# Second attention's weighted values with the tokens on partitions

## The chip, the cores and the metric

The kernel runs on one core of one Trainium2 chip. The metric is the device time of the whole program, in microseconds, the median of several runs. The same program was also run once under the profiler; all rows below are of that one execution.

## The reference

The program takes x (64 sequences of 64 tokens with 128 features, so 4096 tokens) and a context of the same length with 96 features. It adds four layers to x, each on a normalised x: a first attention with a long convolution, a first set of eight experts with two chosen per token, a second attention, and a second set of experts. The change lies in the second attention:

```
qh = (q @ Wq + bq)  -> 16 heads of 8 features
kh = (kv @ Wk + bk) -> 16 heads of 8
vh = (kv @ Wv + bv) -> 16 heads of 8
scores = einsum('bhqd,bhkd->bhqk', qh, kh) * scale
attn = softmax(scores, axis=-1)
out = einsum('bhqk,bhkd->bhqd', attn, vh)   # b, 64 tokens, 16 heads, 8
return out.reshape(b, 64, 128) @ Wo + bo
```

Each of the 64 sequences attends to its own 64 context rows. The layer that follows chooses two of eight experts for each token from logits that the attention's result goes into, so the kernel computes these choices in the same loop, block by block of four tiles.

## The kernel before

The function `combination_and_second_attention` works on 32 tiles of 128 tokens (two sequences each, called b). The engines have their own instruction streams, written out by hand, and meet by semaphores only. Each stream runs a function `slot_of(x)` once for each tile number t (`march`), and inside a slot it works on different tiles, so that the stages of the attention overlap: `a` is tile t+3 (its queries and keys), `g` is tile t+1 (scores, softmax, values), `x` is tile t (its softmax rows are turned), `c` is tile t-1 (weighted values), `d` is tile t-2 (projection and sum).

In one slot, in order:

- TensorE: the scores of g in two halves (L1864; the second half waits for the ScalarE exponentials of the slot before, L2017, as they read the same PSUM tile); the projections of queries and keys of a (L1874, L1875) and of the values of g (L1880), all into the PSUM tile `psx`; in slots 0 to 3 also four small matmuls of logits (L1842); `attend(c)`; once in four slots `ranks` (L1924); `project(d)` (L1931); `turn(x)`, eight transposes of the softmax numerators (L1939).
- ScalarE: the exponentials of g's first half (L2012), the copies of a's keys and queries from `psx` (L2032, L2033), the two copies of g's values into `vb` (L2038), which wait for `attend(c)` because c and g share a `vb` buffer, the exponentials of the second half (L2015, L2017), in some slots the rows for the experts (L2021), and the copies of the turned numerators into `pt` (L2065).
- VectorE: maximum and difference of both halves of g's scores (L2221, L2230), statistics (L2266), `normalise(c)`, which is a reciprocal (L2272) and a product (L2274), `add_result(d)` (L2292), and then, by the slot's number, work on the choice of experts: I call the slots by it. C (t = 3 modulo 4) makes the first choice, D (t = 0) the second, A (t = 1) places the tokens, B (t = 2) has little.
- GpSimd: masked keys for a (L1791), constants, roots, and the indirect DMAs of the expert rows (L1809).

`attend(c)` has the values as the stationary operand: for each of the two sequences and eight pairs of heads a matmul with 32 columns of `vb` (two heads' values in a block of zeros) and 64 columns of `pt` moving, which gives features on partitions. Eight more matmuls with blocks of ones make the sums of the softmax, repeated over the features, in a further 128 columns of the PSUM tile `pso`. `normalise` inverts all 128 x 128 sums and multiplies. Since the result has features on partitions it is at once the stationary operand of the projection.

`normalise(c)` waits not only for `attend(c)` but also for the projection of d in the same slot (`after(dve, s["y"], min(c.t, NT - 2))`), since both use the PSUM tile `pso`. `fill(pe, G, out, n)` elsewhere in the kernel runs n matmuls of a zero tile (128 x 128 with 256 columns moving, L192) whose result nobody reads.

## Time and profile before

| | us |
|---|---|
| median of 3 runs | 920.45 |
| the three runs | 912.15, 920.45, 920.72 |
| the profiled execution | 909.81 |
| its span | 908.6 |
| part of the span with the loop's projections (start of the first in the loop to start of the last) | 572.97 to 735.50 |

The span is the time from the first to the last instruction of the profiled execution; the device time holds 1.2 us more. TensorE is busy in 78% of the span, VectorE in 75%, GpSimd in 62% and ScalarE in 52%, but these are averages over stages with different limits, so the loop is read by itself below. The profiled execution is 1.2% shorter than the median of the three runs, which themselves differ by 0.9%.

### The profile page before, as it was taken

Reading aid. Unit: us, or ns where it says so; the run is one execution under the profiler, and the core shown is the slowest. Engines: PE = TensorE matmul, PEld = TensorE weight load, DVE = VectorE, ACT = ScalarE, POOL = GpSimd, SP = SyncE. Lnnn points to the kernel's source line nnn. Section 1 sums busy time; section 2 is a strip of 40 time slices with the busy share of each in tenths; the row PEclk is TensorE's granted clock in tenths of the full one; section 3 lists DMA queues with packets and bytes.
Section 4 is the critical chain, followed back from the end, with each engine's and each line's share of the span. In section 5 each row is a group of like instructions: output and inputs, shape, how many; then the busy total and the mean of one; then the engine's idle time right before and its main releaser. Section 6 shows DMA issues by size and latency. Waiting matters only on the chain. (4 is left out here: it accounts for less than half of the span.)

```text
span 908.6 us, 21071 instructions
## 1 busy us (share of the span) xinstructions
PE 707.4 (78%) x6384; PEld 522.0 (57%) x6384; DVE 677.9 (75%) x3212; ACT 472.4 (52%) x1318; POOL 565.0 (62%) x932
## 2 busy tenths in 40 slices
PE   0697898899888899943798269988888865899960
PEld 0364565566686566422575256666666642799960
DVE  6798999999447887686111294798998886699964
ACT  3466666765303554520233464777777741677740
POOL 7688977786647443201777684347777767377770
PEclk9879999998999999976899655998988876899985
DMA  6300123777227877500564500000000013799918
GB/s 147 59 25 9 41 49 63 90 93 100 41 47 282 268 253 253 180 1 7 76 122 114 181 28 1 3 2 23 23 26 25 23 34 118 212 274 266 266 53 277
DMA packets 98830, 94.43 MB, mean 104 GB/s; under 512 B 37511, under 2 KB 82302, under 8 KB 98142
## 3 DMA queue, kind: packets, MB, share of 16 engines
q1 hardware_dynamic: 91268, 79.34, 33.1%
q0 software_dynamic: 6592, 13.58, 6.0%
q8 instruction: 52, 0.85, 0.4%
q14 instruction: 60, 0.49, 0.3%
q10 hardware_dynamic: 858, 0.17, 0.1%
HBM read 47.76 MB, written 43.19 MB: 100 GB/s over the span
## 5 line engine op out<-in xcount | busy, mean ns | idle before, releaser
L2455 POOL DMA_INDIRECT expert_pairs<-e_ys,e_home x78 | 75.4, 967 | 38.4 <-issue 23.5
L1791 POOL TENSOR_SCALAR a_kb<-a_kr,a_m,a_bk 128x128 f32<-128x128 f32 x128 | 57.8, 452 | 44.4 <-ACT a_kr L2032 32.3
L1809 POOL DMA_INDIRECT expert_slots<-r_rows,r_slotu x64 | 63.3, 990 | 30.2 <-DVE r_rows L2189 15.1
L961 DVE MATCH_REPLACE8 work<-m,work 128x64 f32<-128x64 f32 x384 | 75.6, 206 | 0.0
L1533 POOL DMA_INDIRECT ex_rows<-rows,slot_source x32 | 30.7, 961 | 53.3 <-POOLq L1176 43.9
L948 DVE MAX8 m<-work 128x8 f32<-128x64 f32 x384 | 57.0, 208 | 0.0
L1864 PE MATMUL a_pss<-a_kb,a_qt 32*64 32x256 f32 x512 | 41.5, 463 | 13.8 <-ACT a_pp L2017 11.7
L2221 DVE TENSOR_REDUCE a_mx<-a_pss 128x8 f32<-128x512 f32 x64 | 43.8, 685 | 8.1 <-PE a_pss L1864 7.8
L2422 PE MATMUL e_ps<-e_XH,e_wh 128*128 128x256 f32 x156 | 48.1, 308 | 1.5 <-DVE e_XL L2467 1.5
L1585 ACT ACTIVATE ex_hs<-ex_psh,vec 128x512 f32<-128x512 f32 x32 | 22.0, 687 | 49.8 <-PE ex_psh L1566 49.1
L2424 PE MATMUL e_ps<-e_XH,e_wl 128*128 128x256 f32 x156 | 44.6, 286 | 0.0
L2423 PE MATMUL e_ps<-e_XL,e_wh 128*128 128x256 f32 x156 | 44.6, 286 | 0.0
L2012 ACT ACTIVATE a_pp<-a_dd 128x512 f32<-128x512 f32 x32 | 20.2, 630 | 45.3 <-DVE a_dd L2230 45.3
L1939 PE MATMUL a_psp<-ident,a_pp 128*128 128x128 f32 x256 | 39.5, 306 | 1.9 <-ACT a_pt L2065 1.9
L2272 DVE RECIPROCAL a_rt<-a_pso 128x128 f32<-128x128 f32 x31 | 29.5, 950 | 14.8 <-PE a_pso L1931 11.9
L209 POOL TENSOR_SCALAR mlp_ln_v<-mlp_ln_mv 128x4 f32<-128x4 f32 x24 | 5.5, 228 | 55.7 <-DVE mlp_ln_mv L201 55.7
L1358 ACT ACTIVATE rt_rs<-mlp_psh,vec 128x512 f32<-128x512 f32 x32 | 22.0, 687 | 34.7 <-PE mlp_psh L1307 34.7
L1543 POOL DMA_INDIRECT planes<-ex_ys,slot_home x32 | 31.2, 975 | 9.9 <-issue 9.4
L834 PE MATMUL psf<-filmw,us 97*128 97x512 f32 x64 | 37.2, 666 | 0.0
L2230 DVE TENSOR_TENSOR a_dd<-a_mx,a_pss 128x512 f32<-128x512 f32 x64 | 35.5, 554 | 2.2
L2065 ACT ACTIVATE a_pt<-a_psp 128x512 f32<-128x512 f32 x64 | 35.4, 610 | 2.2 <-PE a_psp L1939 2.1
L1939 PEld LDWEIGHTS a_psp<-ident,a_pp 128*128 128x128 f32 x256 | 34.8, 161 | 2.5 <-ACT a_pp L2017 2.1
(477 smaller groups left out, 2469.5 us busy)
## 6 DMA issues: line engine op xcount, KB each, us to landing
expert_slots<-rt_unfilled SPq DMA_DIRECT2D x151, 130.0 KB, 2.6
ahead<-folded_weights SPq DMA_DIRECT2D x20, 386.0 KB
e_wf<-folded_weights SPq DMA_DIRECT2D x19, 386.0 KB, 4.1
planes<-rt_zeros SPq DMA_DIRECT2D x4, 1024.0 KB
ew<-in_L_ffn_ew SPq DMA_DIRECT2D x16, 256.0 KB, 3.8
pair_y<-expert_pairs SPq DMA_DIRECT2D x16, 256.0 KB, 5.2
e_xr<-expert_slots SPq DMA_DIRECT2D x27, 130.0 KB, 3.2
folded_weights<-fold_done SPq DMA_DIRECT2D x8, 384.0 KB, 4.3
```

Source lines behind the costliest of these rows:

```text
L834: pe.matmul(psf[:], us[j][:], G.filmw[:], start=True, stop=True).then_inc(s["film"], 1)
L948: mx = dve.max(m8[x.j][:, h, r, :], src[:, h, :])
L961: return own.did(dve.match_replace(wk_[x.j][:, h, :], m8[x.j][:, h, r, :], src[:, h, :], TAKEN))
L1791: m = pool.tensor_scalar(kb[a.j][:, :, h, :], k, m4[:, h:h + 1], bk4[:, h:h + 1], ALU.mult, ALU.add)
L1809: pool.indirect_dma_start(G.slots, bass.IndirectOffsetOnAxis(ap=slot[:, b, k, t:t + 1], axis=0), rb[b % NB][:, k, t, :], None).then_inc(se ...
L1864: mm = pe.matmul(pss[half][T * b:T * b + T, h, 0:HG * T], qt[g.j][rows, T * b:T * b + T], kb[g.j][rows, b, :, :], start=True, stop=True)
L1939: mm = pe.transpose(psp[half][:, k, :], pp[x.j][:, h:h + 2, :].rearrange("p h k -> p (h k)"), G.ident[:])
L2221: dve.tensor_reduce(m, scores(half), AX.X, ALU.min).then_inc(s["lowest"], 1)
L2422: pe.matmul(psh[m][c][:], wh[j][:, m, c, :], XH[j][:], start=True, stop=False)
L2423: pe.matmul(psh[m][c][:], wh[j][:, m, c, :], XL[j][:], start=False, stop=False)
L2424: pe.matmul(psh[m][c][:], wl[j][:, m, c, :], XH[j][:], start=False, stop=True).then_inc(h_ps[m][c], 1)
L2455: pool.indirect_dma_start(G.pair, bass.IndirectOffsetOnAxis(ap=home[i % NY][:, k:k + 1], axis=0), ys[i % NY][:, k, :], None).then_inc(kept ...
```

## The change

The weighted values are made with the softmax numerators as the stationary operand (64 columns, the tokens of one sequence) and 18 columns moving: eight values for each of two heads, and two columns of ones, each over the 64 context rows of one of the heads. 16 matmuls give tokens on partitions, and the two sums of each pair of heads stand beside the values. The eight matmuls of ones are gone. The reciprocal is of 128 x 16 numbers and the product spreads each over eight features. For the projection the result must be turned back: TensorE transposes it in the next slot (`turn_out(d)`, into columns 384 to 511 of `psx`) and ScalarE copies it to a new buffer (`keep_out(d)`), behind its copies of the values of g. `project(d)` waits for that copy. Ahead of `attend(c)` two `fill` matmuls are added. ScalarE's first copies from `psx` also wait for `turn_out(d)`. At the loop's end the order on VectorE changes a little: the last `normalise` stands ahead of `place(LAST - 1)`.

```diff
--- before.py
+++ after.py
@@ -1624,13 +1624,13 @@
         bqs, neg = (C.sb("a1_" + n, [P, 1], ctx=ctx) for n in ("bqs", "neg"))
         m4 = C.sb("a1_m4", [P, HG], ctx=ctx)
         bk4 = C.sb("a1_bk4", [P, HG], ctx=ctx)
-        ones = C.sb("a1_ones", [P, 2, 2, 2, DH1], ctx=ctx)
-
-        vb = two("vb", [P, 2 * NP * 32])
+        VW = 2 * DH1 + 2
+
+        vb = two("vb", [P, 2 * NP, VW])
         qt, kr, kb = two("qt", [P, P]), two("kr", [P, P]), two("kb", [P, 2, HG, T])
         mx, dd, pp = two("mx", [P, H1]), two("dd", [P, H1, T]), two("pp", [P, H1, T])
         pt = two("pt", [P, NP, P])
-        rt, of = two("rt", [P, P]), two("of", [P, P])
+        rt, of, turned_of = two("rt", [P, NP, 2]), two("of", [P, P]), two("ofT", [P, P])
         rb = [C.sb(f"r2_rows{j}", [P, 2, TB, ROW], ctx=ctx) for j in range(NB)]
         full = {n: C.sb("r2_" + n, [P, NT] + k, ctx=ctx) for n, k in (
             ("st", [6]), ("mv", [2]), ("v", []), ("nm", []), ("rstd", []), ("shift", []), ("mc", [NE]), ("lg", [NE]), ("e", [NE]), ("idx", []),
@@ -1669,7 +1669,7 @@
         psl = pso[:, 480:480 + TB * NE]
         s = {n: C.sem("a1_" + n) for n in (
             "ready", "zero", "qkv", "based", "v_sb", "q_sb", "k_sb", "kb",
-            "scores", "lowest", "centred", "exp", "turned", "turned_sb", "inverse", "o", "of", "y", "x", "pool")}
+            "scores", "lowest", "centred", "exp", "turned", "turned_sb", "inverse", "o", "of", "of_turned", "of_sb", "y", "x", "pool")}
         r = {n: C.sem("r2_" + n) for n in (
             "iota", "lg", "var", "root", "rows", "d", "exp", "sel", "ranks", "pos", "counted",
             "slot", "gs", "gturned", "gt", "bias", "bias_sum", "dve", "table")}
@@ -1680,11 +1680,9 @@
         first_weights = [C.later_sem(f"e1_first_weights{i}") for i in range(WEIGHTS_AHEAD)]
         sent = [C.queue_sem(f"r2_sent{j}") for j in range(NB)]
 
-        def vb_rows(j, odd):
-
-            whole = vb[j][:]
-            return bass.AP(whole.tensor, whole.offset + T * odd * whole.ap[0][0] + DH1 * odd,
-                           [[whole.ap[0][0], T], [64, NP], [48, 2], [1, DH1]])
+        def summed(c):
+
+            return outcome(c.t)[:, 0:NP * VW].rearrange("p (k w) -> p k w", w=VW)
 
         def tiles(b):
             return slice(b * TB, (b + 1) * TB)
@@ -1748,10 +1746,9 @@
                 pool.sem_inc(s["zero"], 1)
                 for j in range(2):
                     step.then(pool.memset(vb[j][:], 0.0))
-                step.then(pool.memset(ones[:], 0.0))
-                for pair in range(2):
+                for j in range(2):
                     for odd in range(2):
-                        step.then(pool.memset(ones[T * odd:T * odd + T, pair, pair, odd, :], 1.0))
+                        step.then(pool.memset(vb[j][T * odd:T * odd + T, :, 2 * DH1 + odd:2 * DH1 + odd + 1], 1.0))
                 pool.sem_inc(s["zero"], 1)
                 pool.iota(home_i[:], pattern=[[B * T, 2], [1, NT]], base=0, channel_multiplier=NT).then_inc(r["iota"], 1)
                 pool.iota(tile_i[:], pattern=[[1, NTILE]], base=0, channel_multiplier=0).then_inc(r["iota"], 1)
@@ -1865,6 +1862,7 @@
                                                    kb[g.j][rows, b, :, :], start=True, stop=True)
                             mm.then_inc(s["scores"], 1)
                     if a.real() or g.real():
+                        after(pe, s["of_sb"], d.t)
                         after(pe, s["q_sb"], min(a.t, NT))
                         after(pe, s["v_sb"], min(g.t, NT))
                         if a.real():
@@ -1881,6 +1879,8 @@
                                                    G.ctxT[:, g.t * P + T * b:g.t * P + T * b + T], heads[:, odd],
                                                    start=True, stop=True)
                         mm.then_inc(s["qkv"], 1)
+                    if d.real():
+                        turn_out(d)
                     ranked = due(x, PLACE)
                     if c.real() or ranked is not None:
                         after(pe, cm["base"], min(FIRST + x.t, NBLK))
@@ -1890,6 +1890,7 @@
                     if 0 <= x.t < NBLK - FIRST:
                         base_logits(FIRST + x.t)
                     if c.real():
+                        fill(pe, G, pso[:, 0:2 * P], 2)
                         attend(c)
                     if ranked is not None:
                         ranks(ranked)
@@ -1904,19 +1905,16 @@
                 def attend(c):
                     pe.wait_ge(s["turned_sb"], 2 * c.t + 2)
                     pe.wait_ge(s["v_sb"], c.t + 1)
-                    out = outcome(c.t)
-                    for b in range(2):
-                        for odd in range(2):
-                            for i in range(4):
-                                k = 2 * i + odd
-                                mm = pe.matmul(out[32 * i:32 * i + 32, T * b:T * b + T],
-                                               vb[c.j][:, 32 * (NP * b + k):32 * (NP * b + k) + 32],
-                                               pt[c.j][:, k, T * b:T * b + T], start=odd == 0, stop=odd == 1)
-                    for odd in range(2):
-                        for i in range(4):
-                            mm = pe.matmul(out[32 * i:32 * i + 32, P:2 * P], ones[:, odd].rearrange("p s o d -> p (s o d)"),
-                                           pt[c.j][:, 2 * i + odd, :], start=odd == 0, stop=odd == 1)
+                    out = summed(c)
+                    for k in range(NP):
+                        for b in range(2):
+                            mm = pe.matmul(out[T * b:T * b + T, k, :], pt[c.j][:, k, T * b:T * b + T], vb[c.j][:, NP * b + k, :],
+                                           start=True, stop=True)
                     mm.then_inc(s["o"], 1)
+
+                def turn_out(d):
+                    pe.wait_ge(s["of"], d.t + 1)
+                    pe.transpose(psx[:, 384:512], of[d.j][:], G.ident[:]).then_inc(s["of_turned"], 1)
 
                 def ranks(b):
                     pe.wait_ge(r["sel"], b + 1)
@@ -1926,9 +1924,9 @@
                               start=False, stop=True).then_inc(r["ranks"], 1)
 
                 def project(d):
-                    pe.wait_ge(s["of"], d.t + 1)
+                    pe.wait_ge(s["of_sb"], d.t + 1)
                     out = result(d.t)
-                    pe.matmul(out, of[d.j][:], wo[:], start=True, stop=True).then_inc(s["y"], 1)
+                    pe.matmul(out, turned_of[d.j][:], wo[:], start=True, stop=True).then_inc(s["y"], 1)
 
                 def turn(x):
                     for half in range(2):
@@ -1948,13 +1946,18 @@
                 march(slot_of, -1, NT - 1)
                 t0, t1, t2, t3 = (Tile(t, t // 2, t % 2, True) for t in range(NT - 4, NT))
                 turn(t3)
+                pe.wait_ge(s["v_sb"], NT)
+                pe.wait_ge(s["of_sb"], t1.t)
+                turn_out(t1)
                 pe.wait_ge(s["centred"], 2 * NT)
                 project(t1)
                 pe.wait_ge(s["x"], t0.t + 1)
                 attend(t2)
                 attend(t3)
                 ranks(LAST - 1)
+                turn_out(t2)
                 project(t2)
+                turn_out(t3)
                 pe.wait_ge(s["x"], t1.t + 1)
                 project(t3)
                 pe.wait_ge(s["turned_sb"], 2 * NT)
@@ -2024,8 +2027,11 @@
                 def slot_of(x):
                     a, g = x.by(3), x.by(1)
                     exp(g, 0)
+                    d = x.by(-2)
                     if a.real() or g.real():
                         act.wait_ge(s["qkv"], x.t + 4)
+                        if d.real():
+                            act.wait_ge(s["of_turned"], d.t + 1)
                     if a.real():
                         after(act, s["scores"], 2 * (a.t - 1))
                         after(act, s["kb"], a.t - 1)
@@ -2034,9 +2040,11 @@
                     if g.real():
                         after(act, s["o"], g.t - 1)
                         for odd in range(2):
-                            v = psx[T * odd:T * odd + T, 256:384].rearrange("p (k c d) -> p k c d", c=2, d=DH1)
-                            m = act.activation(vb_rows(g.j, odd), v, ACT.Copy)
+                            v = psx[T * odd:T * odd + T, 256:384].rearrange("p (k d) -> p k d", d=DH1)
+                            m = act.activation(vb[g.j][T * odd:T * odd + T, :, DH1 * odd:DH1 * odd + DH1], v, ACT.Copy)
                         m.then_inc(s["v_sb"], 1)
+                    if d.real():
+                        keep_out(d)
                     if due(x, PLACE) is not None:
                         second_gate(due(x, PLACE))
                     exp(g, 1)
@@ -2064,6 +2072,11 @@
                         act.wait_ge(s["turned"], 2 * x.t + half + 1)
                         act.activation(pt[x.j][:, 4 * half:4 * half + 4, :], psp[half][:], ACT.Copy).then_inc(s["turned_sb"], 1)
 
+                def keep_out(d):
+                    act.wait_ge(s["of_turned"], d.t + 1)
+                    after(act, s["y"], d.t - 1)
+                    act.activation(turned_of[d.j][:], psx[:, 384:512], ACT.Copy).then_inc(s["of_sb"], 1)
+
                 def second_gate(b):
                     act.wait_ge(r["d"], b + 1)
                     act.activation(part(b)["d"], part(b)["d"], ACT.Exp).then_inc(r["exp"], 1)
@@ -2084,15 +2097,20 @@
                 march(slot_of, -1, NT - 1)
                 t0, t1, t2, t3 = (Tile(t, t // 2, t % 2, True) for t in range(NT - 4, NT))
                 keep_turned(t3)
+                keep_out(t1)
                 for b in (LAST - 1, LAST):
                     act.wait_ge(r["root"], b + 1)
                     after(act, sent[b % NB], 2 * TB * 16 * (b // NB))
                     keep_rows(b, 0)
                     keep_rows(b, 1)
                     second_gate(b)
+                    if b < LAST:
+                        keep_out(t2)
                     keep_rows(b, 2)
                     keep_rows(b, 3)
                     keep_places(b)
+                    if b < LAST:
+                        keep_out(t3)
                 for half in range(2):
                     act.wait_ge(r["gturned"], half + 1)
                     act.activation(gt[:, 4 * half:4 * half + 4, :], psp[1][:], ACT.Copy).then_inc(r["gt"], 1)
@@ -2266,12 +2284,15 @@
                     step.did(dve.bn_stats(full["st"][:, n.t, :], G.X[:, n.t, :]))
 
                 def normalise(c):
-                    out = outcome(c.t)
+                    out = summed(c)
                     dve.wait_ge(s["o"], c.t + 1)
                     after(dve, s["y"], min(c.t, NT - 2))
-                    dve.reciprocal(rt[c.j][:], out[:, P:2 * P]).then_inc(s["inverse"], 1)
+                    after(dve, s["of_turned"], c.t - 1)
+                    dve.reciprocal(rt[c.j][:], out[:, :, 2 * DH1:VW]).then_inc(s["inverse"], 1)
                     dve.wait_ge(s["inverse"], c.t + 1)
-                    TT(of[c.j][:], out[:, 0:P], rt[c.j][:], ALU.mult).then_inc(s["of"], 1)
+                    each = [P, NP, 2, DH1]
+                    TT(of[c.j][:].rearrange("p (k o d) -> p k o d", o=2, d=DH1), out[:, :, 0:2 * DH1].rearrange("p k (o d) -> p k o d", o=2),
+                       wide(rt[c.j][:].unsqueeze(3), each), ALU.mult).then_inc(s["of"], 1)
 
                 def means(b):
 
@@ -2307,8 +2328,8 @@
                 add_result(t1)
                 normalise(t2)
                 place_ranks(LAST - 1)
+                normalise(t3)
                 place(LAST - 1)
-                normalise(t3)
                 add_result(t2)
                 for n in (t0, t1, t2):
                     statistics(n)
```

## Rows read from the trace of the kernel before

**Rows 1.** The page, part 2: granted TensorE clock in 40 slices, in tenths.

```profile
PEclk9879999998999999976899655998988876899985
```

**Rows 2.** A round of four slots: us, busy us (instructions) per engine, clock, DMA, GB/s.

```profile
683.44:707.34 23.90, 21.22 (x350) 15.30 (x349) 21.13 (x64) 17.68 (x56) 18.26 (x29) 0.86 0.08 25
```

**Rows 3.** Waits in the loop (566 to 745 us): total us, times, longest.

```profile
DVE a_rt L2272 <- PE a_pso L1931: 11.9, 16, 1.4
```

**Rows 4.** Timeline, slots B and C: start us, us, engine, line, operation [idle before].

```profile
688.10 0.63 ACT L2012 ACTIVATE a_pp<-a_dd 128x512 f32<-128x512 f32 x1 [2.17 <-DVE a_dd L2230]
689.13 0.55 ACT L2038 ACTIVATE a_vb<-a_psx 64x128 f32<-64x128 f32 x2
690.99 0.66 PE L1864 MATMUL a_pss<-a_kb,a_qt 32*64 32x256 f32 x8 [0.67 <-ACT a_pp L2017]
691.58 0.49 PE L1874 MATMUL a_psx<-XF,a_wq 128*128 128x128 f32 x2
692.22 0.45 PE L1880 MATMUL a_psx<-a_wv,ctxT 96*64 96x64 f32 x8
692.60 0.65 PE L1912 MATMUL a_pso<-a_pt,a_vb 128*32 128x64 f32 x32
693.01 0.26 ACT L2032 ACTIVATE a_kr<-a_psx 128x128 f32<-128x128 f32 x1
693.62 0.50 PE L1931 MATMUL a_pso<-a_wo,a_of 128*128 128x136 f32 x2
693.76 0.55 ACT L2038 ACTIVATE a_vb<-a_psx 64x128 f32<-64x128 f32 x2
693.85 0.92 PEld L1939 LDWEIGHTS a_psp<-ident,a_pp 128*128 128x128 f32 x8
694.23 0.96 DVE L2272 RECIPROCAL a_rt<-a_pso 128x128 f32<-128x128 f32 x1 [0.53 <-PE a_pso L1931]
694.93 0.21 PEld L1864 LDWEIGHTS a_pss<-a_kb,a_qt 32*64 32x64 f32 x8 [0.16 <-issue]
695.22 0.29 DVE L2274 TENSOR_TENSOR a_of<-a_pso,a_rt 128x128 f32<-128x128 f32 x1
697.37 0.69 DVE L2221 TENSOR_REDUCE a_mx<-a_pss 128x8 f32<-128x512 f32 x1
```

**Rows 5.** Timeline, slots A and D: VectorE's product and its next maximum.

```profile
684.68 0.29 DVE L2274 TENSOR_TENSOR a_of<-a_pso,a_rt 128x128 f32<-128x128 f32 x1
686.65 0.69 DVE L2221 TENSOR_REDUCE a_mx<-a_pss 128x8 f32<-128x512 f32 x1
700.93 0.29 DVE L2274 TENSOR_TENSOR a_of<-a_pso,a_rt 128x128 f32<-128x128 f32 x1
703.85 0.68 DVE L2221 TENSOR_REDUCE a_mx<-a_pss 128x8 f32<-128x512 f32 x1
```

**Rows 6.** Timeline, TensorE: 64 matmuls with 64 columns stationary between fills (first layer's convolution).

```profile
262.37 0.51 PE L192 MATMUL conv_unread<-still 128*128 128x256 f32 x2
262.81 2.06 PE L1047 MATMUL psy<-XM,toe 64*64 64x32 f32 x64
```

**Rows 7.** Timeline, slot t = 2: logits and values on TensorE, full clock.

```profile
570.96 1.06 PE L1842 MATMUL a_pso<-e_wgt,XF 128*128 128x8 f32 x8
571.95 0.65 PE L1912 MATMUL a_pso<-a_pt,a_vb 128*32 128x64 f32 x32
```

**Rows 8.** The projection's line by itself: ns shortest/median/longest, first and last start in us.

```profile
L1931 PE MATMUL a_pso<-a_wo,a_of x58: 279/383/596, 573.0 to 735.7; 128*128 128x136 f32 x58
```

**Rows 9.** Windows of 1 us around a fall and the next rise of TensorE's clock.

```profile
701.00:702.00 1.00, 0.29 (x8) 0.21 (x8) 0.93 (x6) 1.00 (x4) 0.69 (x2) 1.00 0.18 62
703.00:704.00 1.00, 0.44 (x13) 0.34 (x16) 0.90 (x6) 0.69 (x2) 0.80 (x3) 0.68 0.21 67
710.00:711.00 1.00, 1.00 (x16) 0.67 (x10) 0.90 (x5) 0.00 (x0) 0.00 (x0) 0.91 0.00 0
```

**Rows 10.** Timeline, a small reciprocal in slot A.

```profile
686.16 0.18 DVE L2186 RECIPROCAL r_gate<-r_q 128x4 f32<-128x4 f32 x1
```

**Rows 11.** Timeline, behind the loop: the last reciprocal.

```profile
745.39 0.96 DVE L2272 RECIPROCAL a_rt<-a_pss 128x128 f32<-128x128 f32 x1
```

## The prediction

> **What bounds the kernel now.** I read the page's clock line first, then windows over the loop of the second attention, then its waits, then the timeline of four slots. The clock line [rows 1] shows that the loop (slices 24 to 32) runs at nearly full clock, so the change can't gain by waking TensorE. A round of four slots takes 23.90 us [rows 2], 5.98 a slot, and VectorE is busy for 21.13 of it, TensorE for 21.22: two engines close to their limit. What VectorE lacks is mostly one wait: its 128 x 128 reciprocal stands behind the projection of the same slot, 11.9 us in 16 slots [rows 3]. In slot C one sees it: the projection starts at 693.62 and lasts 0.50, the reciprocal starts at 694.23, 0.11 after its end [rows 4]. Otherwise VectorE runs through: in slot D from its product (700.93) straight to the next maximum (703.85) [rows 5]. So today the loop is VectorE's, with TensorE's projection as the second hand in A and C. The 29 projections of the loop start between 573.0 and 735.5 [rows 8]: 28 intervals, 162.5 us, 5.80 each.
>
> **What the change takes from VectorE.** The reciprocal shrinks from 128 to 16 elements per partition. It takes 0.96 for 128 [rows 4] and 0.18 for 4 [rows 10]; linear between them, 16 take 0.25. With the 0.03 to the product's start that is 0.28 in place of 0.99, 0.7 less per slot. The product keeps its 128 elements and its 0.29. The engine with the most work is relieved by 21 us over 30 slots. What matters is whether it is still the one waited for.
>
> **What it puts on TensorE's path.** The projection used to follow `attend` at once. Now it waits for `keep_out`, which on ScalarE stands behind the two value copies, and these wait for `attend(c)` of the same slot. TensorE works in order, so it stands still through both copies, and the next slot's transposes, scores and projections queue behind it. I add up one round of TensorE, from projection start to projection start, at full clock:
> - projection to the transposes 0.23 (693.62 to 693.85); transposes to the next scores 1.08 (to 694.93); two halves of scores at 0.59 (690.99 to 691.58), 1.18; queries and keys 0.64 (to 692.22); values 0.38 (to 692.60) [rows 4];
> - `turn_out`: two records; the transposes' eight take 0.92 [rows 4], so a quarter, 0.23;
> - the two fills: 0.44 from their start to the next narrow matmul (262.37 to 262.81), in which both changes between full and 64-column matmuls lie [rows 6];
> - the new `attend`: 16 matmuls are 32 records, as the old values' were. The nearest row is the convolution's: 64 records with 64 stationary columns, 2.06 [rows 6]; half is 1.03, and the hop to ScalarE is 0.06, so 1.1;
> - value copies and `keep_out`: the copies take 0.55 [rows 4]; `keep_out` has the shape and source of the key copy, 0.26 [rows 4]; together 0.80, and 0.06 to TensorE, 0.86.
>
> The sum is 0.23 + 1.08 + 1.18 + 0.64 + 0.38 + 0.23 + 0.44 + 1.1 + 0.86 = 6.14. The same sum today is 4.5: no stall, no turn, no fills, and 1.02 for `attend` (692.60 to 693.62 [rows 4]).
>
> Bounds of `attend`, the one large unknown: below, the old values' 32 records, which four column groups share, are all done in 0.65 [rows 7], giving 0.7 and a round of 5.75. Above, if loads of 64 columns don't overlap, half of what full-width loads with 8 columns moving take: 8 records in 0.99 (570.96 to 571.95 [rows 7]), 0.124 each, so 32 x 0.062 = 2.0, with the hop 2.1 and a round of 7.14. I stay with 1.1, since the convolution's form is nearest (same columns, few moving, f32).
>
> The values' records of today come at 0.65 / 32 = 20 ns [rows 7]. The Trainium skill ("TensorE: Matmul & The Clock Gate", section "Wait — 56ns, not 53.3ns?") says that matmuls never start closer than about 25 ns, however few columns move; by that figure `attend` would be 32 x 25 = 0.80, an estimate from that page, and the total 2.4 us less. This trace does not show that floor.
>
> Against the change speaks another rule. What a row shows is 0.65 for values in groups of 32 columns [rows 7]. The Trainium skill ("TensorEngine Tiling (Array Packing)", section "Theoretical Speedup") gives operands of up to 32 columns a factor of four and those of up to 64 only two; twice 0.65 is 1.3, an estimate by that rule, and the total would be 3.7 us more. No run here shows it yet.
>
> **VectorE's path in the new order.** It too passes through the projection, now with ScalarE in it. From a projection's start: its end 0.50, reciprocal 0.11, to the product 0.28, then the stretch X from the product to the next slot's maximum; from there 1.45 to the first exponential (686.65 [rows 5] to 688.10), 1.03 to the value copies (689.13), 0.86 to the next projection [rows 4]: 4.23 + X. X is 1.97 in A (684.68 to 686.65), 2.92 in D [rows 5], 2.15 in C (695.22 to 697.37) [rows 4]. That gives A 6.20, C 6.38, D 7.15; B has no such work and stays below TensorE's round. Both paths run from projection to projection, so each interval is the larger: A 6.20, B 6.14, C 6.38, D 7.15, a round of 25.87 against 23.90. The gain in the reciprocal is spent: VectorE waits longer for the projection than it saves.
>
> **The sum.** Interval 2 to 3 carries the four logit matmuls, 6.14 + 0.99 = 7.13; then four plain ones 24.56; one C 6.38; five rounds 129.35; a D and an A 13.35. Together 180.8 against 162.5: +18.3 (low end +14.4, high end +38.5, by the same sum with 5.75 and 7.14).
> - Slot 1 has no projection yet: its fills, 0.4, ends 0 and 0.5.
> - Behind the loop VectorE is alone for long: two reciprocals, the last at 745.39 with 0.96 [rows 11], save 0.7 each: -1.4. There the added turns and copies fall beside the placing work on VectorE, which now follows the last product; if that cover is gone they cost 1.
> - Clock. It falls once a round, in the slot where TensorE was idle most (busy 0.29 and 0.44 of two of the microseconds before, clock then 0.5) and is back at 710.1, 6.4 us later [rows 9]. Today VectorE hides most of that; with TensorE on the path a fall at the same place would double A's `attend`, turn and fills (1.03 + 0.67, of which D's slack of 7.15 - 6.14 takes 1.0) and its projection and transposes (0.2 + 0.92): about 1.8. Six falls: 10.5; none: 0. The stall now leaves TensorE idle 0.9 of 6.1 in every slot and 1.9 of 7.2 in D, and the fills add work, so the pause is rarer than the one that now precedes a fall; I take 3, nearer to none.
> - Memsets at the start (no 512-wide ones, four thin ones): nothing, as GpSimd is then in the block of sums long before. The waits of ScalarE's key copy for `turn_out(d)`: nothing, the turn is issued right behind the values' matmuls; in B it may be late by 0.2, inside TensorE's round. No DMA is added or moved; GpSimd (18.26 of 23.90 busy [rows 2]) only gets longer slots.
>
> 18.3 + 0.4 - 1.4 + 3 = +20.3. On the profiled execution's 909.8 this is 930.1. That execution lies 10.6 below the median of the runs, 920.45, so on the median it is 941.
>
> **The rivals.**
> - **VectorE stays the bound** (faster). If TensorE's round were under 5.3 (5.98 less 0.7), each slot would shed the reciprocal's 0.7: -21, with the tail -22, 898. For it: 21.13 of 23.90 busy. Against it: five terms of the round without `attend` already give 5.0, and VectorE's own wait is on that projection. 0.07.
> - **No change that can be told.** `attend` at its low end and each hop 0.1 shorter than the rows, 56 hops: 14.4 - 1.0 - 5.6 = +8, 928. 0.13.
> - **Narrow loads don't overlap.** Round 7.14: 38.5 - 1.0 = +37.5, 958. For it: full-width loads are what sets 0.124 today. Against it: the convolution's 0.032. 0.12.
> - **The clock sinks.** The stall in every slot keeps TensorE at half clock in half of the slots. TensorE's own terms, 6.14 - 0.86 = 5.3, would at most double; halfway, +2.5, in 14 slots is 35 more, 976. For it: the stall is new in all slots, and the fall in [rows 9] needed only a few idle stretches. 0.10.
> - That the change doesn't do what it says, say a reciprocal that stays at 0.96, would leave the same stall and add 0.7 to VectorE's path in A, C and D, +12 on the forecast; the row of 0.18 speaks against it. It is within the range and in the forecast's chance.
>
> **How the numbers follow.** Forecast 0.58. A measurement of this kernel can tell about 1% (9.2 us) from no change. Slower by more takes in the forecast, narrow loads and the clock: 0.79. Within 1%: 0.14. Faster: 0.07. The range goes from 922 (low end on a run near the fastest, 912 + 13 = 925, and a part of the second rival) to 963 (past the narrow loads' 958); outside are the faster case and most of the clock's.
>
> **What would show it.** Right: ScalarE's `keep_out` starts right behind the value copies, the projection starts 0.8 to 0.9 after the values' copies began, TensorE's largest wait is that copy; the reciprocal takes about 0.25 and VectorE waits over 1 us ahead of it in nearly every slot; `attend` takes 1.0 to 1.1; a round is 25.9. Wrong: a round at or below 23.9, VectorE without waits, or a projection that starts before the value copies end. A granted clock under 0.8 in the loop would show the fourth rival.

## The result and the profile after

The changed kernel takes 976.3 us (median of four runs, 960.4 to 985.0), the kernel before 917.1 (four runs, 912.2 to 920.7): the ratio is 1.053, with a 95% interval of 1.039 to 1.066. A second set of runs on another occasion gave 975.8 against 921.2, ratio 1.063 (1.054 to 1.071). The ratios leave out runs in a slower state (beside h1 to h4 that is 17 of the 29 runs of the kernel before, whose other 12 have a median of 918.5), so they are not the quotients of the medians. The forecast was 941, which is 2.2% above the kernel before, with a range to 963: the direction was right, the size too small, as 5.3% and 6.3% were measured.

The page of the changed kernel, its clock line and three lines of its part 5 (operation, count | busy us, mean ns | idle before, releaser):

```profile
PEclk9797898979859999965998556787776776799995
L2291 DVE RECIPROCAL a_rt<-a_pso 128x16 f32<-128x16 f32 x31 | 8.0, 258 | 60.8 <-issue 53.7
L1929 PE MATMUL a_pso<-a_wo,a_ofT 128*128 128x136 f32 x58 | 19.5, 432 | 34.8 <-ACT a_ofT L2078 34.5
L1911 PE MATMUL a_pso<-a_vb,a_pt 128*64 128x18 f32 x992 | 40.0, 226 | 0.0
```

The reciprocal has shrunk to 258 ns as forecast. The clock line answers [rows 1]: the loop, slices 24 to 32 before, now shows 6 to 8 where it showed 7 to 9, and the projection L1929 has 34.8 us of idle time ahead of it, ended by the copy of the turned rows.

A round of four slots in the changed kernel, from projection to projection of slot D, by windows (columns as in [rows 2]):

```profile
702.04:732.66 30.62, 25.91 (x296) 20.28 (x297) 19.05 (x64) 18.72 (x60) 18.18 (x30) 0.72 0.06 19
```

30.62 us against 23.90 in [rows 2], with the clock at 0.72. VectorE has 19.05 us of work where it had 21.13, so it sheds 2.1 us and idles 11.6.

The waits of the changed kernel from 566 to 800 us, against [rows 3]:

```profile
DVE a_rt L2291 <- issue: 50.1, 26, 3.6
PE a_pso L1929 <- ACT a_ofT L2078: 33.3, 24, 2.8
DVE a_mx L2239 <- PE a_pss L1861: 25.1, 20, 2.5
```

VectorE's wait ahead of the reciprocal has gone from 11.9 us to 50.1 (put down to "issue", but it ends right behind the projection, 0.09 us in the timeline below). Its wait for scores is 25.1 us; in the kernel before it was at most the 7.8 us of the page's line:

```profile
L2221 DVE TENSOR_REDUCE a_mx<-a_pss 128x8 f32<-128x512 f32 x64 | 43.8, 685 | 8.1 <-PE a_pss L1864 7.8
```

The timeline of slot C at full clock and of the next one, D, which runs at half clock, in the changed kernel:

```profile
692.26 0.14 PEld L1917 LDWEIGHTS a_psx<-ident,a_of 128*128 128x128 f32 x1
692.27 0.36 PEld L192 LDWEIGHTS a_pso<-still 128*128 128x128 f32 x2
692.76 1.11 PE L1911 MATMUL a_pso<-a_vb,a_pt 128*64 128x18 f32 x32
692.89 0.63 ACT L2015 ACTIVATE a_pp<-a_dd 128x512 f32<-128x512 f32 x1 [1.91 <-DVE a_dd L2248]
693.93 0.56 ACT L2044 ACTIVATE a_vb<-a_psx 64x128 f32<-64x128 f32 x2
694.51 0.28 ACT L2078 ACTIVATE a_ofT<-a_psx 128x128 f32<-128x128 f32 x1
694.93 0.47 PE L1929 MATMUL a_pso<-a_wo,a_ofT 128*128 128x136 f32 x2 [1.05 <-ACT a_ofT L2078]
695.49 0.26 DVE L2291 RECIPROCAL a_rt<-a_pso 128x16 f32<-128x16 f32 x1 [1.37 <-issue]
696.20 0.69 PE L1861 MATMUL a_pss<-a_kb,a_qt 32*64 32x256 f32 x16
696.82 0.49 PE L1872 MATMUL a_psx<-XF,a_wq 128*128 128x128 f32 x2
698.34 1.11 PE L1911 MATMUL a_pso<-a_vb,a_pt 128*64 128x18 f32 x32
700.01 0.63 ACT L2015 ACTIVATE a_pp<-a_dd 128x512 f32<-128x512 f32 x1 [2.16 <-DVE a_dd L2248]
701.62 0.28 ACT L2078 ACTIVATE a_ofT<-a_psx 128x128 f32<-128x128 f32 x1
702.04 0.79 PE L1929 MATMUL a_pso<-a_wo,a_ofT 128*128 128x136 f32 x2 [2.58 <-ACT a_ofT L2078]
704.47 1.16 PE L1861 MATMUL a_pss<-a_kb,a_qt 32*64 32x256 f32 x16
706.18 0.69 DVE L2239 TENSOR_REDUCE a_mx<-a_pss 128x8 f32<-128x512 f32 x1
708.17 1.90 PE L1911 MATMUL a_pso<-a_vb,a_pt 128*64 128x18 f32 x32
710.12 0.56 ACT L2044 ACTIVATE a_vb<-a_psx 64x128 f32<-64x128 f32 x2 [1.34 <-PE a_pso L1911]
710.70 0.28 ACT L2078 ACTIVATE a_ofT<-a_psx 128x128 f32<-128x128 f32 x1
711.12 0.79 PE L1929 MATMUL a_pso<-a_wo,a_ofT 128*128 128x136 f32 x2
```

Up to 695 it is what [rows 4] would give with the edit: `attend` 1.11, value copies from 693.93, `keep_out` from 694.51, projection at 694.93. But the projection at 702.04 starts 2.6 us after `attend` is done (698.34 and 1.11): it waits for the copy (701.62), which stands behind an exponential (700.01) that waited for VectorE. From there on everything on TensorE takes almost twice as long, and the next projection comes 9.08 us later.

The distance between projections, split over the run, and where it lies: windows from the first of the loop's 28 intervals to the end of the last, in the kernel before (its second profile) and the changed kernel.

```profile
581.02:744.22 163.20, 143.91 (x2436) 103.96 (x2432) 143.85 (x423) 119.47 (x367) 107.98 (x178) 0.90 0.06 19
```

```profile
601.87:809.48 207.61, 173.79 (x2069) 135.93 (x2069) 128.23 (x425) 127.78 (x398) 108.11 (x177) 0.74 0.05 15
```

So 163.2 us (162.5 in the first profile) became 207.6: +45 between the first profiles, and +46 between the second profiles of both (209.6). Between the second profiles 13.2 us more lie ahead of the loop (581.0 and 594.2 to its first projection), in code that is the same (below). The part behind the 28 intervals is 1 us shorter (173.1 to 172.1), which answers the -1.4 of the forecast.

### The profile page after: what moved, and what is told of

The parts are those of the page before. It is cut to its first block and busy times, and to the rows that moved or that the text cites. A ratio compares the mean times of both kernels' runs of the same rounds, so it can differ in the third digit from the quotient of the medians.

```text
span 981.6 us, 20322 instructions
## 1 busy us (share of the span) xinstructions
PE 760.5 (77%) x5964; PEld 573.8 (58%) x5964; DVE 660.2 (67%) x3212; ACT 481.1 (49%) x1350; POOL 563.9 (57%) x931
## 5 line engine op out<-in xcount | busy, mean ns | idle before, releaser
L1937 PE MATMUL a_psp<-ident,a_pp 128*128 128x128 f32 x256 | 51.4, 368 | 0.4 <-ACT a_pt L2073 0.4
L2291 DVE RECIPROCAL a_rt<-a_pso 128x16 f32<-128x16 f32 x31 | 8.0, 258 | 60.8 <-issue 53.7
L1929 PE MATMUL a_pso<-a_wo,a_ofT 128*128 128x136 f32 x58 | 19.5, 432 | 34.8 <-ACT a_ofT L2078 34.5
L1937 PEld LDWEIGHTS a_psp<-ident,a_pp 128*128 128x128 f32 x256 | 45.8, 198 | 0.7 <-issue 0.6
L1911 PE MATMUL a_pso<-a_vb,a_pt 128*64 128x18 f32 x992 | 40.0, 226 | 0.0
L1911 PEld LDWEIGHTS a_pso<-a_vb,a_pt 128*64 128x64 f32 x992 | 36.9, 157 | 4.9 <-issue 1.8
```

The costliest lines, as they stand in the source:

```text
L1911: mm = pe.matmul(out[T * b:T * b + T, k, :], pt[c.j][:, k, T * b:T * b + T], vb[c.j][:, NP * b + k, :], start=True, stop=True)
L1937: mm = pe.transpose(psp[half][:, k, :], pp[x.j][:, h:h + 2, :].rearrange("p h k -> p (h k)"), G.ident[:])
```

## The experiments

In the table, "intervals" are the 28 distances between projections in the profile, "clock" is the granted clock over them, and the times are medians beside the kernel before on the same chip. The ratio is of the changed version to the kernel before.

| version | us | before | ratio (95%) | intervals | clock |
|---|---|---|---|---|---|
| kernel before, second profile | 918.5 | 918.3 | | 163.2 | 0.90 |
| changed kernel again | 975.8 | 921.2 | 1.063 (1.054 to 1.071) | 209.6 | 0.73 |
| e1: copy at the head of ScalarE's slot | 920.5 | 921.2 | 1.003 (0.996 to 1.011) | 161.1 | 0.92 |
| e2: changed, no fills | 982.5 | 921.2 | none | 211.5 | 0.68 |
| e3: before, with the wait alone | 959.3 | 921.2 | none | 188.5 | 0.84 |
| f1: changed, three value buffers | 963.4 | 918.7 | 1.042 (1.035 to 1.049) | 200.4 | 0.77 |
| f2: f1 without fills | 957.9 | 918.7 | 1.041 (1.034 to 1.049) | 195.8 | 0.70 |
| f3: changed, eight fills in the stall | 965.9 | 918.7 | 1.053 (1.043 to 1.063) | 193.5 | 0.85 |
| f4: before, three value buffers | 917.0 | 918.7 | 0.998 (0.996 to 1.001) | 163.3 | 0.87 |
| g4: changed, transposes ahead of the projection | 963.5 | 918.3 | 1.040 (1.032 to 1.047) | 196.5 | 0.74 |
| g2: e1 with three value buffers | 926.8 | 918.3 | 1.009 (1.005 to 1.012) | 160.4 | 0.91 |
| g3: e1 without fills | 924.3 | 918.3 | 1.006 (1.003 to 1.010) | 159.1 | 0.91 |
| h1: changed, more fills ahead of the convolution | 967.0 | 926.8 | 1.047 (1.040 to 1.053) | 209.6 | 0.73 |
| h3: before, the same | 921.1 | 926.8 | 1.007 (1.002 to 1.011) | 162.7 | 0.88 |
| h2: g2, the same | 916.7 | 926.8 | 0.992 (0.987 to 0.997) | 162.2 | 0.90 |
| h4: h2 without the fills of the loop | 921.1 | 926.8 | 0.998 (0.993 to 1.002) | 162.8 | 0.89 |

**Is it the change, and which part?** The theory: the projection now hangs on ScalarE's copies, TensorE stands still for them, and its clock falls. The rival: the added work on TensorE (turn, fills, matmuls with 64 columns).

The changed kernel again:

> The changed kernel once more, beside runs of the kernel before on the same chip. In its first profile 28.9 us of the 73 us by which the spans differ lie ahead of the loop's first projection, where nothing that costs time was changed, and the loop's projections are 42 us further apart. If the change alone were the cause, the part ahead of the loop would again be 25 to 29 us longer. If that part is a matter of the single run (a clock that falls at other places), it is within 10 us of 573 here, and the total is 30 to 50 us above the kernel before. The intervals between projections should again be some 7.1 in most slots and 5.6 only where the clock is full.

The loop repeats (209.6), and so does the part ahead: the first projection is at 594.2. Neither case written down fits it: it is 21 us later than 573, and 13 later than in the second profile of the kernel before.

The copy moved to the head of ScalarE's slot (e1):

```diff
+                    d = x.by(-2)
+                    if d.real():
+                        keep_out(d)
                     exp(g, 0)
-                    d = x.by(-2)
...
                         m.then_inc(s["v_sb"], 1)
-                    if d.real():
-                        keep_out(d)
```

> The copy of the turned rows moved to the head of ScalarE's slot, ahead of the first exponential and of the copies of the values, so that the projection no longer waits for copies that wait for the weighted values of the same slot. Theory of the stall: TensorE's round loses 0.9 us and its clock holds; VectorE keeps the gain of its small reciprocal; the loop's round of four slots comes to 21 to 24 us and the total within -20 to +5 us of the kernel before, 40 us or more below the changed kernel. Rival, the added work on TensorE (turn, fills, matmuls of 64 columns): the stall was only slack, and the time stays within 10 us of the changed kernel.

920.5 against 921.2: the whole loss of 55 us is gone with all of the added work still in place. In the loop the intervals fall from 209.6 to 161.1; about 10 of the 55 us are a clock ahead of the loop (below). The rival falls: the place of the copy makes the loop's loss, not the added work. The forecast here was the kernel before -20 to +5, and it came out at its upper part. A round of the loop at full clock, and its timeline in slot C:

```profile
671.22:693.44 22.22, 20.92 (x298) 15.47 (x298) 18.60 (x65) 18.74 (x59) 18.35 (x30) 1.00 0.09 27
```

```profile
681.43 0.28 ACT L2078 ACTIVATE a_ofT<-a_psx 128x128 f32<-128x128 f32 x1 [1.06 <-PE a_psx L1917]
681.56 1.11 PE L1911 MATMUL a_pso<-a_vb,a_pt 128*64 128x18 f32 x32
681.60 0.62 ACT L2015 ACTIVATE a_pp<-a_dd 128x512 f32<-128x512 f32 x1
682.61 0.50 PE L1929 MATMUL a_pso<-a_wo,a_ofT 128*128 128x136 f32 x2
682.72 0.56 ACT L2046 ACTIVATE a_vb<-a_psx 64x128 f32<-64x128 f32 x2
```

22.2 us in place of 23.9, with the clock at 1.00 throughout. The copy (681.43 and 0.28) is done 0.15 us after `attend` has begun, the projection (682.61) follows `attend` at once, and the value copies come after it.

The changed kernel without the two fills (e2, the line is left out):

> The changed kernel without the two fill matmuls. Theory of the stall: with the stall in place the fills cost 0.25 to 0.44 us a slot at full clock but keep TensorE a little busier; without them the clock falls as often or more often, the total within 15 us of the changed kernel, either way. Theory of the added work: 0.25 to 0.44 us less at full clock and twice that at half, 30 slots: 10 to 20 us faster.

Within 7 us (982.5, but single runs lie from 964 to 991), the clock of the loop at 0.68 in place of 0.73 and its intervals 2 us longer: less work on TensorE brought nothing that can be told.

The wait alone, in the kernel before (e3):

```diff
                         after(pe, s["x"], d.t)
+                        after(pe, s["v_sb"], min(g.t + 1, NT))
                         project(d)
```

> The kernel before with one part of the change alone: TensorE's projection waits for the copies of the values in the same slot, as it does in the changed kernel by way of the copy behind them. No turn, no fills, no narrow matmuls; the big reciprocal and the ones stay. Theory of the stall: TensorE stands still for 0.65 us in each slot and VectorE's path from projection to projection grows by it: A 6.6, B 5.2, C 6.8, D 7.6 at full clock, a round of 26.3 in place of 23.9, 17 us, and with the clock falling more often 25 to 45 us. Rival, the added work: no more than 5 us above the kernel before.

+38 on the median, +25 in the intervals, with the clock down from 0.90 to 0.84. The profiled run is the shortest of the four (942.6; the others take 958 to 963), so what the others add is not seen. At full clock its slots take 6.54 (A), 5.48 (B), 6.69 (C) and 7.61 (D), within 0.3 of the numbers written down beforehand (C takes 7.39 and 7.71 in two rounds). One wait, without any new work, makes more than half of the loop's loss.

**Which wait inside the chain?** Three buffers for the values take away ScalarE's wait for `attend` of the same slot (f1):

```diff
-        vb = two("vb", [P, 2 * NP, VW])
+        vb = [C.sb(f"a1_vb{j}", [P, 2 * NP, VW], ctx=ctx) for j in range(3)]
...
-                        after(act, s["o"], g.t - 1)
+                        after(act, s["o"], g.t - 2)
...
-                            m = act.activation(vb[g.j][...
+                            m = act.activation(vb[g.t % 3][...
```

> The changed kernel with three buffers for the values in place of two, so that ScalarE's copies of the values, and the copy of the turned rows behind them, no longer wait for the weighted values of the same slot; the order of all instructions stays. Theory of the stall: the wait for attend goes, TensorE stands still at most where VectorE's centred scores are late, the round of four slots falls from about 30 to 22 to 24 us and the 28 intervals from 208 to 150 to 165; the total is 40 to 60 us below the changed kernel and within 10 us of the kernel before. Rival, the added work on TensorE: nothing changes by more than 10 us.

This was wrong: 963.4, intervals 200.4. The timeline of f1 shows why:

```profile
692.49 1.11 PE L1911 MATMUL a_pso<-a_vb,a_pt 128*64 128x18 f32 x32
693.38 0.69 DVE L2248 TENSOR_TENSOR a_dd<-a_mx,a_pss 128x512 f32<-128x512 f32 x1
694.10 0.63 ACT L2015 ACTIVATE a_pp<-a_dd 128x512 f32<-128x512 f32 x1 [2.09 <-DVE a_dd L2248]
695.14 0.55 ACT L2044 ACTIVATE a_vb<-a_psx 64x128 f32<-64x128 f32 x2
695.72 0.28 ACT L2078 ACTIVATE a_ofT<-a_psx 128x128 f32<-128x128 f32 x1
696.14 0.53 PE L1929 MATMUL a_pso<-a_wo,a_ofT 128*128 128x136 f32 x2 [2.53 <-ACT a_ofT L2078]
```

`attend` is done at 693.60, yet the projection waits until 696.14: the copy stands behind the first exponential (694.10), which is released by VectorE's difference (693.38), which VectorE reaches only after the last projection. That is the path I had summed as 4.23 + X. The wait for `attend` was not what bound it.

The same without fills (f2):

> As the one before and without the two fills. If the clock holds by itself once TensorE no longer stands still, the slots that TensorE bounds lose the 0.3 us of the fills: 5 to 9 us below the version with fills. If the fills are what holds the clock, it falls more often and the total is 5 to 30 us above that version.

957.9, 5.5 less at the edge of telling, and a clock of 0.70: neither side is clear.

TensorE's transposes ahead of the projection (g4), so that it has work in the stall:

```diff
-                    if d.real():
-                        after(pe, s["x"], d.t)
-                        project(d)
                     if x.real():
                         ...
                         turn(x)
+                    if d.real():
+                        after(pe, s["x"], d.t)
+                        project(d)
```

> The changed kernel with the eight transposes of the softmax numerators issued ahead of the projection in each slot, so that TensorE has 1.1 us of its own work in the stall. If TensorE's standing still is what costs (through its round, 5.57 us at full clock, and through the clock), the intervals fall from 208 to 165 to 185 and the total by 25 to 45 us. If the path through VectorE and ScalarE is the bound (normalise, maximum, exponential, copies, projection: 6.15, 6.35 and 7.36 in slots A, C and D at full clock), these intervals stay, only B and the early slots gain 0.6 each, 6 us, and what else is gained is clock: 185 to 205.

The second case: intervals 196.5, slots A and C no shorter than in the changed kernel (6.36 at a clock of 0.87, and 6.25 to 7.30 at full clock), the early ones 5.31 in place of 5.57. So it is the ring projection, VectorE, ScalarE, projection that binds in A, C and D, and TensorE's own round only in B and the early slots. But the clock did not come back with the work in the stall. The loops of g4 and of e3, which has the wait and no new work (busy us: TensorE, its loads, VectorE, ScalarE, GpSimd; then the clock):

```profile
599.89:796.39 196.50, 183.05 (x2069) 139.90 (x2069) 126.28 (x425) 124.52 (x397) 108.20 (x177) 0.74 0.05 16
578.49:766.99 188.50, 142.17 (x2432) 106.78 (x2433) 145.66 (x425) 120.20 (x369) 108.86 (x177) 0.84 0.05 17
```

TensorE is busy in 93% of g4's loop at 0.74, and in 75% of e3's at 0.84. So the clock does not follow TensorE's busy share alone, and what in the new order holds it down stays open.

**How much is clock?** Eight more fills in the stall (f3):

```diff
                         after(pe, s["x"], d.t)
+                        for _ in range(8):
+                            pe.matmul(pso[:, NP * VW:2 * P], G.still[:, 0:P],
+                                      G.still[:, 0:2 * P - NP * VW], start=True, stop=True)
                         project(d)
```

> The changed kernel with its stall, and eight more fill matmuls (112 columns moving, into columns of the PSUM tile that nobody reads) in the stall, ahead of the projection. They take about 0.9 us at full clock, as long as the stall. If the clock is the larger part of the loss, the granted clock of the loop rises from 0.74 to over 0.9, the 28 intervals fall from 208 to 175 to 185 (my blind sum without falls gave 181) and the total by 20 to 35 us. If the waiting alone is the loss, whatever the clock, the intervals stay over 200. Where the clock does fall, the fills take 1.8 us and cost up to 0.9 a slot, so 208 to 225.

The clock rose to 0.85 and the intervals fell to 193.5, 14 to 16 less: about half of what was expected, as the clock still fell in D and A (intervals of 10.60, 9.45 and 9.75 at half clock, where the fills cost double). It shows the slots at full clock, though. Intervals with a granted clock of 0.95 or more, in the changed kernel's two profiles and in f3, beside the forecast's:

| slot | forecast | at full clock | at half or mixed, changed kernel |
|---|---|---|---|
| A | 6.20 | 6.07 to 6.18 | 7.13 to 9.09 |
| B | 6.14 | 5.51 to 5.58 | 7.01 to 7.96 |
| C | 6.38 | 6.26 to 7.46 | 7.11 to 7.56 |
| D | 7.15 | 7.36 (one, in f3) | 7.10 to 9.09 |

C has two values. In 15 of the 18 C slots of these three profiles one short VectorE operation takes 0.5 to 1.2 us more than it takes elsewhere, beside GpSimd's addition of the constant, and these slots take 7.06 to 7.56; the three without it take 6.26, 6.30 and 6.35. Two of them in f3, and one in the changed kernel:

```profile
643.91 1.34 POOL L1779 TENSOR_TENSOR X<-X,e_cst 128x544 f32<-128x544 f32 x1
643.93 1.37 DVE L2171 TENSOR_TENSOR r_e<-r_e,iota 128x32 f32<-128x32 f32 x1
700.93 1.34 POOL L1779 TENSOR_TENSOR X<-X,e_cst 128x544 f32<-128x544 f32 x1
700.99 1.32 DVE L2178 SCALAR_TENSOR_TENSOR r_lg<-r_oh,r_lg 128x32 f32<-128x32 f32 x1
```

```profile
696.25 1.33 POOL L1779 TENSOR_TENSOR X<-X,e_cst 128x544 f32<-128x544 f32 x1
696.58 1.06 DVE L2168 TENSOR_TENSOR r_e<-r_lg,r_m 128x32 f32<-128x32 f32 x1
```

With these the 28 intervals at full clock come to 175 to 182 (five early ones at 5.6 with 1 for the logits, six A, five B, six C at 6.3 to 7.3, six D at 7.36), against 163 before. So by this estimate +12 to +19 is the path, and the other 26 to 33 of the 45 are the clock. As nearly every C slot of the changed kernel is a long one, 19 and 26 are the nearer ends. The 163 of the kernel before holds falls of its own (its clock is 0.90), so this compares the changed kernel at full clock with the kernel before as it ran.

Three value buffers in the kernel before (f4):

> The kernel before with three buffers for the values and nothing else of the change. VectorE, with 21.1 of 23.9 us busy in a round, is the bound there, so the theory expects no gain beyond the waits of VectorE for the projection, 0 to 8 us below the kernel before. If the order of the copies was a hidden cost of the kernel before as well, it gains 10 us or more.

917.0 against 918.7: nothing that can be told, which agrees with VectorE as the bound of that loop.

**What lies ahead of the loop?**

> The kernel before, profiled a second time. Its first profile is the only one of ten that reaches the loop's first projection by 573 us; the other kernels' lie at 578 to 602, although their code ahead of the loop is the same. If that part is a matter of the run, this profile lies at 578 to 590 (and some 5 to 15 us of the difference between the first two profiles are no effect of the change); if the changed layout costs there, it lies at 573 again. The 28 intervals of the loop are 162 to 164 either way.

581.0: the first profile of the kernel before was 8 us early at this point by its run. But the changed kernel's 594 and 602 are later still, and one line accounts for it. The convolution of the first layer, L1047, same code in all: durations ns, first to last start, in the second profile of the kernel before, the changed kernel, and h1.

```profile
L1047 PE MATMUL psy<-XM,toe x512: 218/227/248, 258.3 to 277.1; 64*64 64x32 f32 x171
```

```profile
L1047 PE MATMUL psy<-XM,toe x512: 218/291/313, 259.1 to 290.9; 64*64 64x32 f32 x171
```

```profile
L1047 PE MATMUL psy<-XM,toe x512: 218/227/248, 259.9 to 278.8; 64*64 64x32 f32 x171
```

In the changed kernel it takes 31.8 us at a granted clock of 0.53, before 18.8 at 1.00. It does so in both profiles of the changed kernel and in e2, f1, f2, g2 and g4; in both of the kernel before, e1, e3, f3, f4 and g3 it does not. In all seven of the first kind the clock falls 1.9 to 2.8 us after the convolution's start and stays at half for 34 us. More fills ahead of it (h1, and h3 in the kernel before):

```diff
-                fill(pe, G, psa[0][:, 0:256], 12)
+                fill(pe, G, psa[0][:, 0:256], 30)
```

> The changed kernel with 30 in place of 12 fill matmuls between the first layer's attention and its convolution. In both profiles of the changed kernel the clock falls 3 us into the convolution, which then takes 31 us in place of 19. If that fall is a part of the measured difference, the convolution is back at 19 us, the total 10 to 13 us below the changed kernel's 976, at 960 to 966, less up to 2 us for the added fills. If the convolution's clock in a profile says nothing on the timed runs, the total stays at 970 to 978.

967.0, 9 below the changed kernel, a little above the range written down, and the convolution is back at 18.9 us, with the loop's intervals unchanged at 209.6: this clock is a part of the measured difference.

> The kernel before with the same 30 fill matmuls ahead of the convolution. Its convolution ran at full clock in both profiles, so nothing is to be gained: 0 to 2 us above the kernel before. If it gains 5 us or more, its runs fall into both cases as well.

+2.5 on the 918.5 given above, ratio 1.007: it gains nothing. So about 9 to 12 of the 55 us are the convolution's clock, and the loop is the rest. Why the clock falls there with the one kernel and not with the other is open: no instruction up to there is changed (the first that is, GpSimd's clearing of the value buffers, runs at 525 us or later), no run shows a cause, and I tried only the cure.

**Is there a version that is faster?** e1 without fills (g3), and with three value buffers (g2):

> The version with the copy at the head of ScalarE's slot, without the two fills. 0.25 to 0.44 us less per slot on the same ring: 5.15 to 4.8, intervals 151 to 155, the total 6 to 10 us below that version and below the kernel before by 5 to 10. If the fills are what holds the clock at full there, it falls again in the slots D and A and the intervals are 162 to 175.

> The version with the copy of the turned rows at the head of ScalarE's slot, and three buffers for the values. At full clock that version's slots B and C took 5.15 us, the ring exponential, scores, projections of queries, keys and values, attend, value copies, exponential. Without the wait of the value copies for attend the ring loses up to 0.4 us and TensorE's own round of 4.9 decides: 28 intervals 150 to 160 in place of 161, the total 2 to 10 us below that version. If the clock falls more often, since TensorE has less to do per us, no gain.

g3: 159.1 us of intervals but 924.3: not faster. g2: 160.4, at the upper end, and 926.8, with the convolution at half clock. With that mended (h2, and h4 without the fills of the loop):

> The version with the copy of the turned rows at the head of ScalarE's slot and three buffers for the values, with the 30 fill matmuls. In its profile the loop took 160.4 us, 2.8 less than the second profile of the kernel before, but the convolution ran at half clock. With that gone 927 falls to 912 to 917, 2 to 6 us below the kernel before. If it stays above 922, the clock moves elsewhere.

> As the one before without the two fills ahead of the weighted values. TensorE's round is then 4.6 us at full clock and VectorE's work, 18.3 us in four slots, comes close: 28 intervals 145 to 157, the total 905 to 915. If TensorE idles so much that the clock falls, intervals 160 to 170 and a total at or above the kernel before.

h2 takes 916.7 with a ratio of 0.992 (0.987 to 0.997), the lowest of all versions. But it lies only 1.8 us under the 918.5 given above, and the kernel before had medians of 917.1 to 921.2 on other occasions: a gain of under 1%, which these runs do not settle, and no version is shown to be clearly faster. h4 is the same as before within its interval. Part of what e1 should have gained goes to the loop's start: in its profile slots 8 to 10 take 8.40, 7.97 and 6.70 at a falling clock, while the later rounds take 22.

## Why the prediction was right or wrong

- **The bound.** Right: VectorE bounded the loop, and its wait for the projection was the hinge. It sheds 2.1 us a round (21.13 to 19.05; forecast 2.8, where the one operation that is long beside GpSimd's addition, 1.00 in this round, takes 0.8 back) and gains nothing.
- **The reciprocal** at 0.25: measured 0.258.
- **`attend`** at 1.03, and 1.1 to ScalarE: it takes 1.11 at full clock, 1.17 to ScalarE (692.76 to 693.93), and 1.90 at half clock. The Trainium skill ("TensorEngine Tiling (Array Packing)", section "Theoretical Speedup") had led to an estimate of 1.3; the trace is below it. (By the forecast's own sum, that estimate would have cost 3.9 us and not 3.7.) The Trainium skill ("TensorE: Matmul & The Clock Gate", section "Wait — 56ns, not 53.3ns?") had led to one of 0.80, which was too low by more; the 20 ns a record of [rows 7] had already been under its 25 ns.
- **TensorE's round** 6.14: measured 5.57. Too large in two terms: the turn is one record (0.14), and the two halves of scores take 0.62 together when the second need not wait (696.20 to 696.82), where I took 0.59 twice. One term was too small: from the value copies' start to the projection it is 1.00 (693.93 to 694.93), not 0.86.
- **VectorE's path**, A 6.20, C 6.38, D 7.15: 6.07 to 6.18, 6.26 to 7.46, 7.36. Right where VectorE's operations keep their length, and f1 and g4 show that it is this path that binds. The forecast let GpSimd cost nothing; its addition now lies beside a short VectorE operation in nearly every C slot and costs 0.8 to 1.2 there, about 5 us in six rounds. The prose ahead of it blamed the copies' wait for `attend`; taking that away (f1) gave 12 of 55.
- **The sum at full clock**, +18.3: the profiles' slots give +12 to +19. Right, in part by luck, as TensorE's round was taken too long and the C slots too short.
- **The clock**, "I take 3, nearer to none", ends 0 and 10.5: this is the step that failed. It measured 26 to 33. I reasoned that short pauses and two fills would make falls rarer than one a round. In fact the loop's granted clock is 0.74 and 0.73 in the two profiles, which is half of the time at half clock, in 14 and 12 stretches where the sum had six at most; 21 and 22 of the 28 intervals have a clock below 0.95. D runs mostly at half clock and A, B and C in part. By [rows 9] a fall lasts 6.8 us and not 6.4, as the 0.68 and 0.91 put its ends at 703.4 and 710.2. The price of one fall, 1.8, was nearer: 26 to 33 over 12 to 14 stretches is 2 to 3 each, D goes from 7.36 to 9.08 and B from 5.57 to 7.1 (a stretch that spans a slot slows projection, transposes, scores and `attend`, which lie in series in the ring). TensorE idles in 16% of the loop (173.8 of 207.6 busy; before 11%), but e3 and g4 show that this share alone does not set the clock, so why it stays down is open.
- **The fourth rival** had the clock at half in half of the slots, at 976, with a chance of 0.10, and the prediction's own sign of it, a granted clock under 0.8, came. The evidence for it, a stall that is new in every slot, stood in its own sentence and should have had the larger share. That its 976 is also the measured median is luck: it charged the loop 35 us of clock on top of the forecast, the loop took 23 to 30 more than the forecast's 3, and the convolution, which the prediction did not have, added 9 to 12.
- **Outside the loop.** The sum had no term for the part ahead of the loop; it is off by 9 to 12 us in the measured runs, by a clock in the convolution that no step of mine touched. The end of the loop, -1.4, came at -1.0.

## What to carry to other kernels

When a change hands an engine's result through another engine's queue, look where in that queue the hand-over stands: here the same copy made the loop 45 us longer behind the exponentials and no longer ahead of them. Sum the ring at half clock too, if TensorE will pause in every turn of it, and give the outcome in which the clock stays down a price and a chance of its own. The clock can also fall in a stage that the change does not touch, as in the convolution here, so compare the stages that should be the same first. And look beside which instructions of the other engines a moved operation now lies: the C slots grew by about 1 us that way.

## What the runs showed of the hardware

- The clock of the same convolution fell in some kernels and not in others, with the same instructions: 31.1 to 31.8 us in seven profiles, 18.8 in seven.
- The loop ran at 0.74 and 0.73 of the full clock with TensorE busy in 84% of the time, with no wait for a copy longer than 2.9 us; e1, busy in 153.96 of 161.1 us (96%), ran at 0.92. Busy share alone does not order the versions: e3 ran at 0.84 with 75%, g4 at 0.74 with 93%.
- The same 32 records of `attend` took 1.11 us at full clock and 1.90 at half.
- A VectorE operation on 128 x 32 elements took up to 1.38 us where it mostly takes 0.16 to 0.23, while GpSimd's addition of the constant (1.33 us) ran beside it. It was not always the same operation (L2307 and L2168 in the changed kernel, L2171 and L2178 in f3 too), and in all 15 cases of the changed kernel's two profiles and f3 it ended 0.05 us after the addition did, as in the pairs shown above (696.58 and 1.06 is 697.64; 696.25 and 1.33 is 697.58). VectorE's maxima and differences, which read PSUM, kept their 0.69 us beside the same addition. No version moved the addition away, so that it is the cause is told by this timing and not by an experiment.
